# Row sums of the attention weights taken over pairs of tiles, added on VectorE first

## Chip, cores and metric

One Trainium2 chip, all 8 cores, one launch. Each core computes 1024 of the 8192 rows (batch x position) of the output; the cores don't talk to each other. The metric is the device time in microseconds (us) of the slowest core.

## The reference

One transformer layer, postnorm: strictly causal attention with 16 query heads over one shared key/value head, layer norm of the sum with the input, then a gated FFN with a Walsh-Hadamard transform of the hidden layer, and a second layer norm. Of it the attention is what matters here:

```python
q = (q_input @ Wq.T + bq).reshape(B, T, 16, 128).transpose(0, 2, 1, 3)   # B=2, T=4096
k = q_input @ Wk.T + bk                                                  # 128 wide, one head
v = q_input @ Wv.T + bv
mask = pos[None, :] < pos[:, None]
scores = jnp.einsum('bhtd,bsd->bhts', q, k) * scale
scores = jnp.where(mask[None, None, :, :], scores, NEG_BIG)
attn = jax.nn.softmax(scores, axis=-1)
...
out = jnp.einsum('bhts,bsd->bhtd', attn, v)
```

The softmax's denominator is the sum over s of exp(score); the kernel subtracts no maximum.

## The kernel before

The program is written out by hand: `em.op(engine, fn, waits)` appends an instruction to one engine's list ("t" TensorE, "v" VectorE, "s" ScalarE, "g" and "y" the GpSimd and SyncE queues for DMAs) and gives back a token, the value of that engine's semaphore after it. The lists are replayed in that order, so each engine runs its instructions in program order, and a wait holds all that stands behind it in its list. `inc=False` gives an instruction no token.

Stages in order: keys and values with W2T transforms (`p0_step`) woven in, queries, attention, output projection, first norm, FFN up, FFN down, second norm. All matmuls but those of `p0_step` go through line 177, whatever they compute; those of `p0_step` through 179.

The attention stage runs from about 334 to 1092 us. It loops over k = 0..7 (blocks of 128 queries) and g = 0..3 (groups of 4 heads): 32 groups, here counted by (k, g). A group works on 4(k+1) tiles; a tile is 128 keys by 512 columns (4 heads x 128 queries), held transposed with the keys on the partitions. The stage has 576 tiles. For each tile:

- QK: a matmul of kT and qT into one of two PSUM banks (of four, once the 64 `p0_step`s are done, from k=4 on);
- for the last four tiles of a group, those on the diagonal, a mask is added in PSUM on VectorE (L430);
- ScalarE takes the exp into a slot of `pbuf`, bf16, 128x512 (L433), six slots in turn;
- AV: a matmul of vP and the slot, accumulated over the group in bank 2 or 3;
- RS: a matmul of the one-column ONEC and the slot, accumulated in bank 4, row 0: the row sum.

AV and RS of a tile are issued two tiles behind its QK (`pend`). At the end of a group the last two are drained, and VectorE runs r1 (L446), r3 (L450), r4 (L452) and r5 (L454) on the row sum: it is split in two bf16 parts in RB2. What follows from it, `fin`, is issued in the next group, at it == 2, behind QK(2) and ahead of AV(0): two matmuls b1 and b2 that broadcast the two parts over the partitions (they wait for r3 and r5), the reciprocal on VectorE (L471) and the multiplication of the group's AV sum with it (L475). After the drain each group calls `p0_step` twice until the 64 are used up; at an odd step VectorE moves its results out of PSUM (L244), at an even one ScalarE (L240).

`pbuf` is laid out as eight slots of 1 KB, of which six are used. `pbuf_rd[slot]` holds the token for which the next exp into the slot waits.

Of the kernel before, what the change touches and what calls it, by code (L numbers as in the profile page):

```python
# [55 lines left out]
def _mx(*toks):  # L56
    d = {}

    def add(u):
        if u[0] in "gy":  # L60
            k = (u[0], ((u[1] // 16) - 1) % NL)
        else:
            k = u[0]
        if d.get(k, 0) < u[1]:
            d[k] = u[1]

    for t in toks:
        if not t:
            continue
        if isinstance(t, list):  # L70
            for u in t:
                if u:
                    add(u)
        else:
            add(t)
    return [((k[0] if isinstance(k, tuple) else k), v) for k, v in d.items()]


def build_program():
# [23 lines left out]
    em = EM()  # L103

    import contextlib
    with contextlib.ExitStack() as stack:
# [16 lines left out]
        pb = [ent(nc.psum_tensor("pb%d" % i, [128, 512], F32)) for i in range(8)]  # L123
# [32 lines left out]
        pbuf = [vb(O_PB + i * 1024, 512) for i in range(8)]  # L156
# [15 lines left out]
        ONEC = CB[:, 320:321]  # L172
        ONER = CB[0:1, 320:448]

        def MM(e, out, lhsT, rhs, start, stop, tp=None):
            if tp is None:
                return e.matmul(out, lhsT, rhs, start=start, stop=stop,  # L177
                                skip_group_check=True)
            return e.matmul(out, lhsT, rhs, start=start, stop=stop,  # L179
                            skip_group_check=True, tile_position=tp)  # L180

        tCB = em.op("y", lambda e: e.dma_start(CB[:], CONSTI[:]))
# [8 lines left out]
        for cc in range(4):  # L191
            sl = slice(cc * 512, cc * 512 + 512)
            tw = em.op("y", lambda e, sl=sl: e.dma_start(RR[0:1, 0:512], BOR[0:1, sl]),
                       waits=_mx(rr_rd))
            t1 = em.op("v", lambda e, sl=sl: e.tensor_sub(RR[0:1, 512:1024], RR[0:1, 0:512], BO2[0:1, sl]),
                       waits=_mx(tw, tBOh, last))
            rr_rd = t1
            last = em.op("v", lambda e, cc=cc: e.tensor_copy(BO2[0:1, 2048 + cc * 512:2048 + cc * 512 + 512], RR[0:1, 512:1024]),
                         waits=_mx(t1))
# [73 lines left out]
        for blk in range(8):  # L273
# [4 lines left out]
                waits=_mx(xtb_rd[sl]))  # L278
            pk = pb[sl]
            mmk = None  # L280
            for c in range(DC):
# [4 lines left out]
                    waits=_mx(tl, tWK, ps_tok[sl]) if c == 0 else (),  # L286
# [3 lines left out]
                waits=_mx(mmk, tBK))  # L290
# [4 lines left out]
            for c in range(DC):  # L295
# [4 lines left out]
                    waits=_mx(tWV, ps_tok[2 + sl]) if c == 0 else (),  # L300
# [4 lines left out]
                waits=_mx(mmv, tBV, vT_rd[sl]))  # L305
            ps_tok[2 + sl] = tev
            for st in range(4):
# [6 lines left out]
                    waits=_mx(tev, tCB, ps_tok[bank]))  # L314
                tevt = em.op("s", lambda e, pt=pt, sig=sig: e.copy(
                    vP[:, sig * 128:sig * 128 + 128], pt[:, 0:128]),
                    waits=_mx(mmt))
# [16 lines left out]
        for oq in range(4):  # L334
            sl = oq % 2
            tl = em.op("g", lambda e, sl=sl, oq=oq: e.dma_start(wqb[sl], WQS[oq]),
                       waits=_mx(wq_rd[sl]))
            for ot in range(4):
# [3 lines left out]
                for c in range(DC):  # L342
                    for th in range(2):
# [5 lines left out]
                            waits=_mx(tl, tXTOWN, q_ps_rd[bset + th]) if c == 0 else (),  # L349
# [29 lines left out]
        attnT_wr = []  # L379
        sig_ctr = 0  # L380
        first_attnT = True
        st3 = {"rb_rd": rb_rd, "rb2_rd": rb2_rd, "fin": None}

        qctr = 0
        for k in range(J):
            for g in range(NG):
                if p0_state["i"] >= 64 and len(QKB) == 2:
                    QKB = (0, 1, 6, 7)
                    qk_rd[6] = ps_tok[6]
                    qk_rd[7] = ps_tok[7]  # L390
                    qctr = 0
                avbank = 2 + (g % 2)
                avp = pb[avbank]
                rs_mm = None
                pend = []
                niter = (k + 1) * 4
                it = 0

                def emit_avrs(slot, sig, first, last_av, texp,
                              avp=avp, avbank=avbank):  # L400
                    em.op("t", lambda e, avp=avp, slot=slot, sig=sig,
                          first=first, last_av=last_av: MM(
                        e, avp[:], vP[:, sig * 128:sig * 128 + 128], pbuf[slot],
                        first, last_av),
                        waits=_mx(texp, tVP, av_rd[avbank] if first else None),
                        inc=False)
                    rs = em.op("t", lambda e, slot=slot, first=first,
                               last_av=last_av: MM(
                        e, pb[4][0:1, :], ONEC, pbuf[slot], first, last_av),
                        waits=_mx(rs_rd, tCB) if first else ())  # L410
                    pbuf_rd[slot] = rs
                    return rs

                for c in range(k + 1):
                    for q4 in range(4):
                        sig = 4 * c + q4
                        bank = QKB[qctr % len(QKB)]
                        qctr += 1
                        slot = sig_ctr % 6
                        sig_ctr += 1  # L420
                        qp = pb[bank]
                        rhs = qT.rearrange("p (h x) -> p h x", x=1024)[
                            :, 4 * g:4 * g + 4, k * 128:k * 128 + 128]
                        mm = em.op("t", lambda e, qp=qp, sig=sig, rhs=rhs: MM(
                            e, qp[:], kT[:, sig * 128:sig * 128 + 128], rhs,
                            True, True),
                            waits=_mx(tKT, tQT, qk_rd[bank]))
                        dep = mm
                        if c == k:
                            dep = em.op("v", lambda e, qp=qp, q4=q4: e.tensor_add(  # L430
                                qp[:], qp[:], maskP[:, q4 * 512:q4 * 512 + 512]),
                                waits=_mx(mm, tMask))
                        texp = em.op("s", lambda e, qp=qp, slot=slot: e.activation(  # L433
                            pbuf[slot], qp[:], AF.Exp, scale=SC),
                            waits=_mx(dep, pbuf_rd[slot]))
                        qk_rd[bank] = texp
                        if it == 2 and st3["fin"] is not None:
                            st3["fin"]()
                            st3["fin"] = None
                        if len(pend) == 2:  # L440
                            rs_mm = emit_avrs(*pend.pop(0))
                        pend.append((slot, sig, it == 0, it == niter - 1, texp))
                        it += 1
                while pend:
                    rs_mm = emit_avrs(*pend.pop(0))
                r1 = em.op("v", lambda e: e.tensor_scalar_add(RR[0:1, 0:512], pb[4][0:1, :], 1e-30),  # L446
                           waits=_mx(rs_mm, rr_war[0]))
                rr_war[0] = None
                rs_rd = r1
                r3 = em.op("v", lambda e: e.tensor_copy(RB2[0:1, 0:512], RR[0:1, 0:512]),  # L450
                           waits=_mx(r1, st3["rb2_rd"][0]))
                r4 = em.op("v", lambda e: e.tensor_sub(RR[0:1, 512:1024], RR[0:1, 0:512], RB2[0:1, 0:512]),  # L452
                           waits=_mx(r3))
                r5 = em.op("v", lambda e: e.tensor_copy(RB2[0:1, 512:1024], RR[0:1, 512:1024]),  # L454
                           waits=_mx(r4, st3["rb2_rd"][1]))
                rsl = (k * NG + g) % 2
                dst = attnT.rearrange("p (h x) -> p h x", x=1024)[
                    :, 4 * g:4 * g + 4, k * 128:k * 128 + 128]

                def make_fin(avp=avp, avbank=avbank, rsl=rsl, dst=dst,  # L460
                             rs_mm=rs_mm, r3=r3, r5=r5, fat=first_attnT,
                             qlm=q_last_mm):
                    def fin():
                        em.op("t", lambda e: MM(
                            e, pb[5][:], ONER, RB2[0:1, 0:512], True, False),
                            waits=_mx(r3, st3["rb_rd"]), inc=False)
                        b2 = em.op("t", lambda e: MM(
                            e, pb[5][:], ONER, RB2[0:1, 512:1024], False, True),
                            waits=_mx(r5))
                        st3["rb2_rd"] = [b2, b2]  # L470
                        vrec = em.op("v", lambda e, rsl=rsl: e.reciprocal(  # L471
                            recB[rsl], pb[5][:]),
                            waits=_mx(b2, recB_rd[rsl]))
                        st3["rb_rd"] = vrec
                        tv = em.op("v", lambda e, avp=avp, rsl=rsl, dst=dst: e.tensor_mul(  # L475
                            dst, avp[:], recB[rsl]),
                            waits=_mx(rs_mm, vrec, qlm if fat else None))
                        av_rd[avbank] = tv
                        recB_rd[rsl] = tv
                        attnT_wr.append(tv)  # L480
                    return fin

                st3["fin"] = make_fin()
                first_attnT = False
                p0_step()
                p0_step()
# [430 lines left out]
```

How the kernel before makes its waits and increments, by code:

```python
            def run(eng):  # L791
                lastw = {}
                def wait_tok(sc, val):
                    if sc in "gy":
                        n = val // 16
                        l = (n - 1) % NL
                        lv = 16 * ((n - 1) // NL + 1)
                        key = (sc, l)
                        if lastw.get(key, -1) < lv:
                            eng.wait_ge(lanes[sc][l], lv)
                            lastw[key] = lv
                    else:
                        if lastw.get(sc, -1) < val:
                            eng.wait_ge(sems[sc], val)
                            lastw[sc] = val
                for fn, ws, tok in em.ops[eng_char]:
                    if ANALYZE is not None:
                        ANALYZE(eng_char, fn, ws, tok)
                    for (sc, val) in ws:
                        wait_tok(sc, val)
                    if tok is not None and tok[0] in "gy":
                        n = tok[1] // 16
                        if n > NL:
                            wait_tok(tok[0], 16 * (n - NL))
                    ins = fn(eng)
                    if tok is not None:
                        if tok[0] in "gy":
                            n = tok[1] // 16
                            ins.then_inc(lanes[tok[0]][(n - 1) % NL], 16)
                        else:
                            ins.then_inc(sems[tok[0]], 1)
```

## Time and profile before

| | us |
|---|---|
| median of 3 runs | 2852.98 |
| the runs | 2852.71 to 3084.56 |
| the profiled execution | 2852.75 |
| its span, slowest core (first to last instruction) | 2851.2 |
| spans of the eight cores | 2840.8 to 2851.2 |

The profile shows the slowest core, 6. "PE" is a matmul on TensorE, "DVE" VectorE, "ACT" ScalarE. Duration of a matmul is from its start to a modelled end; the next one starts earlier, so the pace is read from the starts. "[0.70 <-DVE RB L450]" is the idle time of that engine ahead of the row and what ended it. "PEclk" is the granted TensorE clock as a share of its upper level: 1.00 is 2.4 GHz, 0.50 is 1.2 GHz.

### The profile page before, as it was taken

Reading aid. Unit: us, or ns where it says so; the run is one execution under the profiler, and the core shown is the slowest. Engines: PE = TensorE matmul, PEld = TensorE weight load, DVE = VectorE, ACT = ScalarE, POOL = GpSimd, SP = SyncE. Lnnn points to the kernel's source line nnn. Section 1 sums busy time; section 2 is a strip of 40 time slices with the busy share of each in tenths; the row PEclk is TensorE's granted clock in tenths of the full one; section 3 lists DMA queues with packets and bytes.
Section 4 is the critical chain, followed back from the end, with each engine's and each line's share of the span. In section 5 each row is a group of like instructions: output and inputs, shape, how many; then the busy total and the mean of one; then the engine's idle time right before and its main releaser. Section 6 shows DMA issues by size and latency. Waiting matters only on the chain.

```text
span 2851.2 us, 27832 instructions; the slowest of 8 cores (2840.8 to 2851.2 us)
## 1 busy us (share of the span) xinstructions
PE 2407.6 (84%) x9884; PEld 911.2 (32%) x10080; DVE 552.1 (19%) x768; ACT 647.7 (23%) x1131; POOL 162.8 (6%) x304
## 2 busy tenths in 40 slices
PE   3778758788889897957999999999999997979793
PEld 1233211112212222323444444444444443434341
DVE  1111346544332321131000000000000000010002
ACT  1222223445555551033111111111111100000001
POOL 1111101100000000000000000000000000000000
PEclk8799957889989998978999999999999998989896
DMA  8875554430000001122222212222222145446453
GB/s 235 235 210 155 168 165 118 113 91 18 1 1 0 1 1 59 60 103 86 69 67 69 71 67 68 73 67 67 74 67 67 52 140 148 144 138 199 133 153 126
DMA packets 96460, 276.69 MB, mean 97 GB/s; under 512 B 11716, under 2 KB 11844, under 8 KB 91976
## 3 DMA queue, kind: packets, MB, share of 16 engines
q0 software_dynamic: 37968, 156.26, 18.4%
q1 hardware_dynamic: 58360, 118.65, 13.5%
q8 instruction: 86, 1.41, 0.2%
q14 instruction: 46, 0.38, 0.0%
HBM read 224.54 MB, written 50.33 MB: 96 GB/s over the span
## 4 chain that ended last, share of the span: by engine, by line
PE 77%; DMA 7%; ACT 5%; DVE 5%; issue 5%; ACTq 0%; POOL 0%; DVEq 0%; SPq 0%; POOLq 0%
PE pb L177 75%; DMA GA<-XBT 2%; PE pb L179 2%; DMA GA<-X1S 2%; ACT GA L677 1%; ACT GA L433 1%; DVE pb L430 1%; DMA W2P<-GA 1%; ACT GA L240 1%; DVE GA L244 1%; DMA GA<-W2P 1%; DVE GA L471 1%; ACT GA L558 1%; DVE GA L737 0%; DVE RR L452 0%
## 5 line engine op out<-in xcount | busy, mean ns | idle before, releaser
L177 PE MATMUL pb<-GA 128*128 128x512 bf16 x8382 | 2045.4, 390 | 211.9 <-DVE GA L737 50.1
L177 PEld LDWEIGHTS pb<-GA 128*128 128x128 bf16 x8576 | 798.9, 99 | 1327.8 <-issue 505.2
L433 ACT ACTIVATE GA<-pb 128x512 bf16<-128x512 f32 x576 | 339.1, 597 | 336.0 <-PE pb L177 239.0
L177 PE MATMUL pb<-GA,CB 128*1 128x512 bf16 (+1 forms) x702 | 275.2, 406 | 13.7 <-issue 6.0
L677 ACT ACTIVATE GA<-pb 128x512 bf16<-128x512 f32 x128 | 69.6, 594 | 840.6 <-PE pb L177 840.5
L657 DVE TENSOR_TENSOR GA<-GA,pb 128x512 bf16<-128x512 f32 x128 | 82.3, 683 | 902.8 <-ACT GA L654 883.6
L179 PE MATMUL pb<-GA,CB 64*64 64x512 bf16 x512 | 107.9, 444 | 85.4 <-ACT GA L240 55.2
L177 PEld LDWEIGHTS pb<-GA,CB 128*1 128x1 bf16 (+1 forms) x704 | 58.1, 82 | 278.2 <-issue 263.4
L430 DVE TENSOR_TENSOR pb<-pb,GA 128x512 f32<-128x512 f32 x128 | 88.6, 698 | 296.8 <-PE pb L177 289.2
L244 DVE CAST GA<-pb 128x512 bf16<-128x512 f32 x128 | 82.6, 686 | 279.7 <-PE pb L179 278.4
L737 DVE TENSOR_TENSOR GA<-pb,GA 128x512 f32<-128x512 f32 x32 | 20.6, 686 | 497.3 <-PE pb L177 435.3
L471 DVE RECIPROCAL GA<-pb 128x512 f32<-128x512 f32 x32 | 107.4, 3357 | 36.2 <-PE pb L177 36.2
L179 PEld LDWEIGHTS pb<-GA,CB 64*64 64x64 bf16 x512 | 31.6, 108 | 159.2 <-issue 159.0
L240 ACT CAST GA<-pb 128x512 bf16<-128x512 f32 x128 | 68.7, 588 | 52.7 <-PE pb L179 31.1
L177 PE MATMUL pb<-CB,GA 128*128 128x128 bf16 x160 | 22.0, 285 | 59.9 <-ACT GA L565 36.8
L654 ACT ACTIVATE GA<-pb 128x512 f32<-128x512 f32 x128 | 70.0, 609 | 0.0
L617 POOL DMA_DIRECT2D GA<-W1S x64 | 34.0, 531 | 615.6 <-PE pb L177 605.1
L217 POOL DMA_DIRECT2D GA<-W2T x64 | 33.2, 518 | 543.2 <-PE pb L179 505.8
L762 ACT ACT_TABLE_LOAD x1 | 1.3, 1283 | 268.3 <-DVE LNS L760 268.3
L762 ACT ACTIVATE LNS<-LNS,EPSB 128x1 f32<-128x1 f32 x8 | 2.3, 292 | 252.9 <-DVE LNS L760 252.9
L619 POOL DMA_DIRECT2D GA<-W3S x64 | 34.0, 531 | 395.5 <-PE pb L177 392.7
L177 PE MATMUL pb<-RB,CB 1*128 1x512 bf16 x64 | 28.9, 500 | 26.8 <-DVE RB L454 14.9
(48 smaller groups left out, 382.8 us busy)
## 6 DMA issues: line engine op xcount, KB each, us to landing
GA<-W2P SPq DMA_DIRECT2D x256, 256.0 KB, 2.7
GA<-W2T POOLq DMA_DIRECT2D x128, 256.0 KB, 4.9
W2P<-GA SPq DMA_DIRECT2D x128, 256.0 KB, 5.9
GA<-W1S POOLq DMA_DIRECT2D x64, 512.0 KB, 3.7
GA<-W3S POOLq DMA_DIRECT2D x64, 512.0 KB, 3.7
GA<-XBT POOLq DMA_DIRECT2D x8, 2048.0 KB, 16.6
GA<-WQS POOLq DMA_DIRECT2D x4, 2048.0 KB, 11.8
GA<-XOWN SPq DMA_DIRECT2D x1, 8192.0 KB, 37.9
```

Source lines behind the costliest of these rows:

```text
L177: return e.matmul(out, lhsT, rhs, start=start, stop=stop, skip_group_check=True)
L179: return e.matmul(out, lhsT, rhs, start=start, stop=stop, skip_group_check=True, tile_position=tp)
L240: te = em.op("s", lambda e, ps=ps, stb=stb, q4=q4: e.copy(stb[:, q4 * 512:q4 * 512 + 512], ps[:]), waits=_mx(tm, p0_state["st_rd"][j % 2]))
L244: te = em.op("v", lambda e, ps=ps, stb=stb, q4=q4: e.tensor_copy(stb[:, q4 * 512:q4 * 512 + 512], ps[:]), waits=_mx(tm, p0_state["st_rd"][ ...
L430: dep = em.op("v", lambda e, qp=qp, q4=q4: e.tensor_add(qp[:], qp[:], maskP[:, q4 * 512:q4 * 512 + 512]), waits=_mx(mm, tMask))
L433: texp = em.op("s", lambda e, qp=qp, slot=slot: e.activation(pbuf[slot], qp[:], AF.Exp, scale=SC), waits=_mx(dep, pbuf_rd[slot]))
L471: vrec = em.op("v", lambda e, rsl=rsl: e.reciprocal(recB[rsl], pb[5][:]), waits=_mx(b2, recB_rd[rsl]))
L617: tl1 = em.op("g", lambda e, sl=sl, tau=tau: e.dma_start(w1b[sl], W1S[tau]), waits=_mx(w1_rd[sl]))
L619: tl3 = em.op("g", lambda e, sl=sl, tau=tau: e.dma_start(w3b[sl], W3S[tau]), waits=_mx(w3_rd[sl]))
L654: ts_ = em.op("s", lambda e, pg=pg, sl=sl, th=th: e.activation(silu[sl][:, th * 512:th * 512 + 512], pg[:], AF.Silu), waits=_mx(g_toks[th] ...
L657: tvm = em.op("v", lambda e, pl=pl, sl=sl, th=th: e.tensor_mul(hbuf[sl][:, th * 512:th * 512 + 512], silu[sl][:, th * 512:th * 512 + 512], ...
L677: ev = em.op("s", lambda e, pg=pg, tau=tau, th=th: e.activation(hid[:, tau * 1024 + th * 512:tau * 1024 + th * 512 + 512], pg[:], AF.Ident ...
```

## The change

RS is no longer taken of each tile. When AV of the second tile of a pair has been issued, VectorE adds the two `pbuf` slots into a third, slot 6 or 7 in turn, and one RS is taken of that sum. The sum is bf16, as are its inputs. The RS waits for the addition; the addition waits for both exps and for the RS that last read its slot. A slot of the first six is given free when both the addition and that RS are done. 288 RS matmuls stay, 288 additions are new. Nothing else is changed.

```diff
-        st3 = {"rb_rd": rb_rd, "rb2_rd": rb2_rd, "fin": None}
+        st3 = {"rb_rd": rb_rd, "rb2_rd": rb2_rd, "fin": None, "pc": 0}
+        pbuf6_rd = [None, None]
...
+                rsp = []
...
                         waits=_mx(texp, tVP, av_rd[avbank] if first else None),
                         inc=False)
-                    rs = em.op("t", lambda e, slot=slot, first=first,
-                               last_av=last_av: MM(
-                        e, pb[4][0:1, :], ONEC, pbuf[slot], first, last_av),
-                        waits=_mx(rs_rd, tCB) if first else ())
-                    pbuf_rd[slot] = rs
+                    rsp.append((slot, texp, first, last_av))
+                    rs = None
+                    if len(rsp) == 2:
+                        (sa, ta_, fa, la_), (sb, tb_, fb, lb_) = rsp
+                        del rsp[:]
+                        psl = 6 + (st3["pc"] % 2)
+                        st3["pc"] += 1
+                        va = em.op("v", lambda e, sa=sa, sb=sb, psl=psl: e.tensor_add(
+                            pbuf[psl], pbuf[sa], pbuf[sb]),
+                            waits=_mx(ta_, tb_, pbuf6_rd[psl - 6]))
+                        rs = em.op("t", lambda e, psl=psl, fa=fa, lb_=lb_: MM(
+                            e, pb[4][0:1, :], ONEC, pbuf[psl], fa, lb_),
+                            waits=_mx(va, rs_rd, tCB) if fa else _mx(va))
+                        pbuf6_rd[psl - 6] = rs
+                        pbuf_rd[sa] = _mx(rs, va)
+                        pbuf_rd[sb] = _mx(rs, va)
                     return rs
...
                         if len(pend) == 2:
-                            rs_mm = emit_avrs(*pend.pop(0))
+                            rs_mm = emit_avrs(*pend.pop(0)) or rs_mm
...
                 while pend:
-                    rs_mm = emit_avrs(*pend.pop(0))
+                    rs_mm = emit_avrs(*pend.pop(0)) or rs_mm
```

## Rows read from the trace of the kernel before

**Rows 1.** The page, part 4, the chain that ended last, by engine.
```profile
PE 77%; DMA 7%; ACT 5%; DVE 5%; issue 5%; ACTq 0%; POOL 0%; DVEq 0%; SPq 0%; POOLq 0%
```
**Rows 2.** Busy time by window, attention stage: from:to, length, engines, PEclk, DMA share, GB/s.
```profile
334.00:1092.00 758.00, 634.14 (x2007) 140.91 (x2046) 324.30 (x383) 373.48 (x640) 31.12 (x61) 0.85 0.20 56
```
**Rows 3.** Groups by line and form: operation, shapes, count | busy, mean ns | idle before.
```profile
L177 PE MATMUL pb<-GA,CB 128*1 128x512 bf16 x576 | 237.4, 412 | 10.8 <-issue 6.0 <-ACT GA L433 1.8
...
L430 DVE TENSOR_TENSOR pb<-pb,GA 128x512 f32<-128x512 f32 x128 | 88.6, 698 | 296.8 <-PE pb L177 289.2
...
L452 DVE TENSOR_TENSOR RR<-RR,RB 1x512 f32<-1x512 f32 x32 | 21.7, 679 | 3.3
...
L450 DVE CAST RB<-RR 1x512 bf16<-1x512 f32 x32 | 13.3, 415 | 3.3
```
**Rows 4.** Timeline, all engines, mid-group (k=7): start, duration, engine, operation, count.
```profile
1000.02 0.38 PE L177 MATMUL pb<-GA,CB 128*1 128x512 bf16 x1
...
1000.33 0.60 PE L177 MATMUL pb<-GA 128*128 128x512 bf16 x2
1000.81 0.60 ACT L433 ACTIVATE GA<-pb 128x512 bf16<-128x512 f32 x1 [0.25 <-PE pb L177]
...
1000.86 0.38 PE L177 MATMUL pb<-GA,CB 128*1 128x512 bf16 x1
```
**Rows 5.** Timeline, first masks on the diagonal of that group.
```profile
1018.56 1.54 DVE L430 TENSOR_TENSOR pb<-pb,GA 128x512 f32<-128x512 f32 x2 [19.39 <-PE pb L177]
```
**Rows 6.** Timeline, end of that group and head of the next.
```profile
1023.41 0.82 PE L177 MATMUL pb<-GA 128*128 128x512 bf16 x3
1023.59 0.68 DVE L446 TENSOR_SCALAR RR<-pb 1x512 f32<-1x512 f32 x1 [1.68 <-PE pb L177]
...
1025.67 0.41 DVE L454 CAST RB<-RR 1x512 bf16<-1x512 f32 x1
...
1026.23 0.58 PE L177 MATMUL pb<-RB,CB 1*128 1x512 bf16 x1 [0.93 <-DVE RB L454]
...
1026.92 3.36 DVE L471 RECIPROCAL GA<-pb 128x512 f32<-128x512 f32 x1 [0.83 <-PE pb L177]
...
1028.76 0.58 PE L177 MATMUL pb<-GA,CB 128*1 128x512 bf16 x1
...
1030.24 0.58 PE L177 MATMUL pb<-GA,CB 128*1 128x512 bf16 x1
1030.38 0.69 DVE L475 TENSOR_TENSOR GA<-pb,GA 128x512 bf16<-128x512 f32 x1
```
**Rows 7.** Busy time by window, columns as in rows 2; two low stretches and k=4.
```profile
995.50:998.90 3.40, 3.40 (x9) 0.51 (x8) 3.29 (x2) 1.19 (x2) 0.00 (x0) 0.50 0.03 7
...
1026.20:1033.00 6.80, 6.77 (x14) 1.03 (x14) 4.05 (x2) 1.85 (x4) 0.00 (x0) 0.50 0.00 0
...
705.30:742.90 37.60, 33.44 (x115) 8.11 (x116) 14.67 (x20) 22.70 (x39) 0.00 (x0) 1.00 0.00 1
```
**Rows 8.** Timeline of VectorE: reciprocals and r1 in groups of k=2, 4, 7.
```profile
546.38 3.36 DVE L471 RECIPROCAL GA<-pb 128x512 f32<-128x512 f32 x1 [1.94 <-PE pb L177]
...
559.13 0.68 DVE L446 TENSOR_SCALAR RR<-pb 1x512 f32<-1x512 f32 x1 [1.68 <-PE pb L177]
...
702.12 3.36 DVE L471 RECIPROCAL GA<-pb 128x512 f32<-128x512 f32 x1 [0.62 <-PE pb L177]
...
720.55 0.68 DVE L446 TENSOR_SCALAR RR<-pb 1x512 f32<-1x512 f32 x1 [1.68 <-PE pb L177]
723.67 3.36 DVE L471 RECIPROCAL GA<-pb 128x512 f32<-128x512 f32 x1 [0.62 <-PE pb L177]
...
740.63 0.68 DVE L446 TENSOR_SCALAR RR<-pb 1x512 f32<-1x512 f32 x1 [1.68 <-PE pb L177]
...
995.01 3.36 DVE L471 RECIPROCAL GA<-pb 128x512 f32<-128x512 f32 x1 [0.62 <-PE pb L177]
...
1056.71 0.68 DVE L446 TENSOR_SCALAR RR<-pb 1x512 f32<-1x512 f32 x1 [1.68 <-PE pb L177]
```

## The prediction

> **What bounds the kernel now.** I read the page first. Its chain of work that ended last lies on TensorE [rows 1], so a change off TensorE counts only through what TensorE waits for. The busy time by window comes next: the attention stage holds 758 of 2851 us, TensorE busy in 634 of them, ScalarE in 373, VectorE in 324 [rows 2]. The groups by form give the price of each operation there, among them the 576 row-sum matmuls of which the change takes half away [rows 3]. Then the timeline, in four places. In the middle of a group TensorE is the pace: a tile (scores QK, weighted values AV, row sum RS) recurs every 0.84 us, and the exp takes 0.60 of it [rows 4]. On the diagonal four masks stand on VectorE, and 5.03 us pass from the first mask to r1 [rows 5, 6]. Between groups TensorE waits for r1 to r5, runs the two broadcast matmuls of `fin` and goes on, while VectorE works off the reciprocal (3.36 us) and the multiplication (0.69) behind which nobody waits [rows 6]. In some of these places the granted clock falls to 1.2 GHz for 3.4 or 6.8 us, and a tile then takes 1.48 us instead of 0.84; in others it stays at 2.4 GHz [rows 7, 6].
>
> **What a removed row sum is worth.** RS starts, QK starts 0.31 later, AV follows, and the next RS starts 0.53 after that QK [rows 4]. Three QKs in a row take 0.82 with a last duration of 0.39, so matmuls of one shape stand 0.216 apart [rows 6]. Each change of shape to the one-column weights and back costs about 0.09 more. A tile without its RS is therefore 0.844 - 0.31 - 0.31 + 0.216 = 0.44, a pair with one RS 0.844 + 0.44 = 1.286, or 0.643 per tile. One removed RS gives 0.40 us, 288 of them 116 us, if nothing waits. At the low clock I scale the tile: 1.48 x 0.643 / 0.844 = 1.13 us. ScalarE at 0.60 stays just under that pace.
>
> **What the new addition costs.** The trace has no addition of bf16 with bf16. Its nearest rows at 512 elements: TENSOR_TENSOR f32 in SBUF 679 ns, with PSUM 698, CAST f32 to bf16 415 [rows 3]. The addition reads 2+2 bytes and writes 2 per element, as the cast reads 4 and writes 2, while the f32 addition moves 12; I take 0.415 us and keep 0.68 for the upper end. Less than 0.415 no row suggests. With 0.415 the sum below comes to 2924 us, with 0.68 to 2969.
>
> Beside that, the Trainium skill ("VectorE: DVE Perf Modes", The perf-mode tier table) puts tensor_tensor on bf16 in SBUF at two elements a cycle, 1224 ns for 2048 elements; less three quarters of the elements, that is an estimate of 424 ns here. By it the sum would be 2925 us. No row of this trace shows a two-source operation at that rate.
>
> In the middle of a group the addition is hidden. Handover from matmul to exp is 0.48 (1000.33 to 1000.81), the exp 0.60 [rows 4], a handover from ScalarE to VectorE 0.10 (my estimate; TensorE to VectorE takes about as long as TensorE to ScalarE, and VectorE to TensorE 0.15), the addition 0.415, and one to TensorE 0.15 (L454 ends 1026.08, broadcast 1026.23) [rows 6]: 1.75 us after its QK the sum is there. RS(pair) stands 1.82 us behind the QK of its second tile (one pair period of 1.286, plus 0.53). 0.07 us to spare, and at 0.68 a wait of 0.19 per pair.
>
> **Where it isn't hidden: at the head of a group.** `fin` is emitted at it == 2, and its reciprocal and multiplication enter VectorE's queue. The first pair's addition is emitted at it == 3, behind both, and VectorE works in order. RS(0,1) stands in TensorE's queue right behind AV(1), and behind it QK(4), so all of the group. Counted from the start of the reciprocal: multiplication from 3.46 to 4.15 [rows 6], addition to 4.6, RS(0,1) at 4.75. TensorE has by then done AV(0), QK(3), AV(1), four matmuls' work with the broadcast, and idles for about 3 us. In the kernel before it works through at that place. QK(4) follows at 5.29 (0.31 scaled to the low clock).
>
> The clock: a gap of this size next to that of r1 to r5 leaves it at 1.2 GHz. Before, low stretches were 3.4 or 6.8 us long [rows 7]; I take 5.1 us from RS(0,1), so until 9.85. In it (9.85 - 5.29) / 1.13 = 4.0 tiles pass: QK(8) at 9.85, and from there 0.643 per tile.
>
> **And on the diagonal.** With T the start of the first mask (QK + 0.49; the masks take 0.70): second mask T+0.66 to 1.36, then the addition of the pair before to 1.74, its RS 1.88 (TensorE waits 1.4 us), the next two QKs 2.19 and 2.62, masks 2.67 to 3.37 and 3.33 to 4.03, the second addition to 4.41, its RS 4.55, last exp 4.13 to 4.73, last AV 5.07, last addition 4.83 to 5.25, last RS 5.39, r1 5.88. Before it was 5.03. So from QK of the first masked tile to r1: 0.49 + 5.88 = 6.37. pbuf is no new wait: a slot is used again six tiles on, a pair frees it after three.
>
> **The sum.** Reciprocal to r1 for U unmasked tiles, after: 9.85 + (U - 8) x 0.643 + 6.37, and for U = 4 5.29 + 6.37 = 11.7. Before, from the reciprocal and r1 of [rows 8] and [rows 6]: k=2 12.75; k=4 18.43 and 16.96, mean 17.7; k=7 28.58 and 29.79, mean 29.2; the others a tile rate of 0.844 away from a neighbour.
> U = 4 (k=1): 11.7 against 9.4, +2.3. U = 8: 16.2 against 12.75, +3.45. U = 12: 18.8 against 16.1, +2.7. U = 16: 21.35 against 17.7, +3.65. U = 20: 23.9 against 22.4, +1.5. U = 24: 26.5 against 25.8, +0.7. U = 28: 29.05 against 29.2, -0.15. Together 14.15, times four groups: +56.5. k=0: three groups with a `fin` whose last mask waited for the reciprocal already, +0.35 each (0.10 + 0.415 + 0.15 less 0.31), +1. The saving of the row sums is inside these figures; every fourth tile is on a diagonal or in the low stretch, where it is eaten.
> To it: TensorE idles about 3 of the 5.9 us of the diagonal, so I let the clock fall there in half of the 28 groups, 0.8 us each (the last four matmuls twice as long): +11. The two broadcasts at the low clock, 0.2 us in 14 more groups: +3. Sum +71.5. The profiled execution ran 2852.75 us (span 2851.2; the median of the runs is 2852.98): 2924 us. The stages behind are not touched, and the W2T transforms (L179), whose VectorE casts stand ahead of the reciprocal, keep their place in each queue and so their price: 0.
>
> **The rivals.**
> A. The low stretch after the stall is always 3.4 us and none falls on the diagonal: 1.7 x (1 - 0.643/1.13) = 0.73 us in 24 groups less, 2852.75 + 57.5 - 17.5 = 2893. For it: of the two late groups shown one has the short stretch [rows 7]. Against: in those the work behind the broadcasts was without a gap, and here the stall lies in it.
> B. Not slower: the clock stays at 2.4 GHz through the stall. Then QK(4) comes at 5.06 and U = 4..28 give +2.0, +1.25, +0.5, +1.5, -0.7, -1.5, -2.3, times four +3, with k=0 +4: 2857. It decides at the head of each group. For it: one boundary at k=4 was crossed at 2.4 GHz [rows 7]. Against: that gap was 2 us, here there are two with 5 us of idling in 7.
> C. The addition takes 0.68: 0.26 more at the head, 0.52 on the diagonal, 28 times, 22 us; and 0.19 in the 120 pairs at full clock, 23 us: 2969. For it: each two-source row is at 679 or more. Against: the bytes moved.
> D. The reciprocal doesn't hold the sum up and the whole 116 us are gained: 2737. The program's order speaks against it; nothing for it.
>
> **How the numbers follow.** The forecast has 0.57, A 0.17, B 0.08, C 0.14, D 0.04. About 2% (2910 us) is what a measurement here can tell from no change. The forecast's own spread is 2900 to 2950, so one tenth of it lies within 2%, as do A and B: same 0.31. Faster 0.05, D and some of B. Slower 0.64. The range 2880 to 2975 takes in the forecast, A and C, and leaves out B and D.
>
> **What would show it right or wrong.** The mean of the new addition (415 ns). A wait of TensorE for it once per group of about 3 us behind the multiplication, 28 times, some 85 us in all, and two of 1 to 1.5 us on the diagonal. Tiles 1.29 us per pair in mid-group at 2.4 GHz. A granted clock of the attention stage under the 0.85 of before. Reciprocal to r1 near 16 us at k=2 and 29 at k=7. Wrong would be: no wait at the head (D), or a clock of 1.00 there (B). The stages behind should not change.

## The result, and the profile after

| | before | after |
|---|---|---|
| ratio to the kernel before | 1 | 1.0253 (95% interval 1.0225 to 1.028) |
| median of all runs, us | 2863.19 (10 runs) | 2926.68 (10 runs) |
| profiled execution, us | 2852.75 | 2930.88 |
| its span, slowest core, us | 2851.2 (core 6) | 2929.2 (core 1) |

The change makes the kernel 2.5% slower: 1.0253 times the 2852.98 us of the runs shown is 2925 us, where 2924 was predicted. In some runs the cores of one die show a lower granted clock and the time is longer, whatever the kernel; the ratios, here and below, leave these runs out.

The spans differ by 78 us and the whole runs by 72: eleven microseconds of the difference lie ahead of attention (first exp at 345.1 us here, at 334.2 before) where the program is the same. In this execution cores 0 and 1 were granted less clock there (PEclk, third from the end, is 0.70 in core 1 and 0.82 in core 2), and their first exp comes at 344.0 and 345.1 us, that of the other six at 322.3 to 335.8. Window 62 to 220 us, core 1 and then core 2:

```profile
62.00:220.00 158.00, 125.73 (x461) 45.29 (x462) 20.64 (x32) 38.03 (x83) 24.51 (x41) 0.70 0.75 213
```
```profile
62.00:220.00 158.00, 126.24 (x509) 47.74 (x508) 23.21 (x36) 39.39 (x85) 25.61 (x43) 0.82 0.77 216
```

From the first reciprocal to the last, attention takes 811.8 us instead of 744.4, 67.4 more; on the mean of the eight cores it is 68.7.

The chain of work that ended last, by engine and by line (compare [rows 1]): VectorE goes from 5% to 10%, and the reciprocal (L484, before L471) from 1% to 4%; it now stands second.

```profile
PE 74%; DVE 10%; DMA 6%; issue 5%; ACT 5%; DVEq 0%; ACTq 0%; POOL 0%; SPq 0%; POOLq 0%
PE pb L177 71%; DVE GA L484 4%; PE pb L179 2%; DVE pb L443 2%; DMA GA<-XBT 2%; DMA GA<-X1S 2%; ACT GA L690 1%; DVE GA L416 1%; ACT GA L240 1%; DMA W2P<-GA 1%; DVE GA L244 1%; DMA GA<-W2P 1%; ACT GA L571 1%; ACT GA L446 1%; DVE GA L750 0%
```

The windows of the kernel after (columns as in [rows 2]): the attention stage, then a stretch in k=0 and k=1, then two low stretches of k=7. TensorE has 66 us less work and the stage is 69 us longer; the granted clock over it falls from 0.85 to 0.74. From the first r1 to the last, 423 of 818 us are at 1.2 GHz, where it was 225 of 750.

```profile
345.00:1172.00 827.00, 568.50 (x1758) 139.38 (x1758) 432.00 (x670) 358.22 (x640) 30.89 (x61) 0.74 0.17 51
...
1101.10:1114.70 13.60, 8.88 (x19) 1.66 (x20) 7.80 (x12) 4.18 (x8) 0.00 (x0) 0.50 0.00 0
...
1138.60:1148.90 10.30, 6.96 (x16) 1.51 (x16) 5.37 (x6) 2.98 (x5) 0.00 (x0) 0.50 0.00 0
346.70:524.20 177.50, 108.44 (x278) 21.62 (x277) 99.88 (x137) 48.88 (x86) 16.35 (x32) 0.50 0.48 147
```

Groups by form and the waits of TensorE in that kernel: the halved row sums with the idle time in front of them (10.8 us before, [rows 3]), the addition (L416), and the sum of TensorE's waits for an addition, with their number and the longest. The first row sums of the 28 groups from k=1 on hold 101 us of that idle time, 3.34 to 3.98 us each.

```profile
L177 PE MATMUL pb<-GA,CB 128*1 128x512 bf16 x288 | 127.4, 443 | 183.2 <-DVE GA L416 180.9
...
L416 DVE TENSOR_TENSOR GA<-GA 128x512 bf16<-128x512 bf16 x288 | 119.5, 422 | 209.3 <-PE pb L177 119.0
```
```profile
PE pb L177 <- DVE GA L416: 180.9, 94, 4.0
```

The head of a group of k=7, timeline of all engines. It answers to [rows 6]. The two additions at 1111.27 come when the multiplication L488 is done; RS(0,1) follows at 1111.83, after 3.35 us in which TensorE had nothing.

```profile
1106.51 0.58 PE L177 MATMUL pb<-RB,CB 1*128 1x512 bf16 x1 [0.72 <-DVE RB L467]
...
1107.02 1.46 PE L177 MATMUL pb<-GA 128*128 128x512 bf16 x3
...
1107.20 3.36 DVE L484 RECIPROCAL GA<-pb 128x512 f32<-128x512 f32 x1 [0.83 <-PE pb L177]
...
1110.66 0.69 DVE L488 TENSOR_TENSOR GA<-pb,GA 128x512 bf16<-128x512 f32 x1
1111.27 0.75 DVE L416 TENSOR_TENSOR GA<-GA 128x512 bf16<-128x512 bf16 x2
...
1111.83 0.59 PE L177 MATMUL pb<-GA,CB 128*1 128x512 bf16 x1 [3.35 <-DVE GA L416]
```

Mid-group in the same kernel: row sums at 1122.58, 1123.86 and 1125.26, so a pair takes 1.28 and 1.40 us in turn.

```profile
1122.58 0.38 PE L177 MATMUL pb<-GA,CB 128*1 128x512 bf16 x1
...
1123.86 0.38 PE L177 MATMUL pb<-GA,CB 128*1 128x512 bf16 x1
...
1125.26 0.38 PE L177 MATMUL pb<-GA,CB 128*1 128x512 bf16 x1
```

The diagonal of that kernel, TensorE, and VectorE's first mask and r1 (it answers to [rows 5, 6]): two waits of 1.23 us for additions that stand behind masks, and 5.73 us from first mask to r1 instead of 5.03. These two waits stand in each group from k=2 on; in k=1 they are of 0.85 us.

```profile
1131.79 0.38 PE L177 MATMUL pb<-GA,CB 128*1 128x512 bf16 x1 [1.23 <-DVE GA L416]
1132.10 1.04 PE L177 MATMUL pb<-GA 128*128 128x512 bf16 x4
1134.36 0.38 PE L177 MATMUL pb<-GA,CB 128*1 128x512 bf16 x1 [1.23 <-DVE GA L416]
```
```profile
1130.02 1.30 DVE L443 TENSOR_TENSOR pb<-pb,GA 128x512 f32<-128x512 f32 x2 [0.95 <-PE pb L177]
...
1135.75 0.68 DVE L459 TENSOR_SCALAR RR<-pb 1x512 f32<-1x512 f32 x1 [0.63 <-PE pb L177]
```

### The profile page after: what moved, and what is told of

The parts are those of the page before. It is cut to its first block, busy times and chain, and to the rows that moved or that the text cites. A ratio compares the mean times of both kernels' runs of the same rounds, so it can differ in the third digit from the quotient of the medians.

```text
span 2929.2 us, 28624 instructions; the slowest of 8 cores (2904.3 to 2929.2 us)
## 1 busy us (share of the span) xinstructions
PE 2363.5 (81%) x9792; PEld 911.1 (31%) x9792; DVE 660.0 (23%) x1056; ACT 632.7 (22%) x1131; POOL 162.1 (6%) x304
## 3 DMA queue, kind: packets, MB, share of 16 engines
q1 hardware_dynamic: 58360, 118.65, 12.7%
## 4 chain that ended last, share of the span: by engine, by line
PE 74%; DVE 10%; DMA 6%; issue 5%; ACT 5%; DVEq 0%; ACTq 0%; POOL 0%; SPq 0%; POOLq 0%
PE pb L177 71%; DVE GA L484 4%; PE pb L179 2%; DVE pb L443 2%; DMA GA<-XBT 2%; DMA GA<-X1S 2%; ACT GA L690 1%; DVE GA L416 1%; ACT GA L240 1%; DMA W2P<-GA 1%; DVE GA L244 1%; DMA GA<-W2P 1%; ACT GA L571 1%; ACT GA L446 1%; DVE GA L750 0%
## 5 line engine op out<-in xcount | busy, mean ns | idle before, releaser
L177 PE MATMUL pb<-GA 128*128 128x512 bf16 x8576 | 2056.4, 395 | 175.7 <-DVE GA L750 45.9
L177 PEld LDWEIGHTS pb<-GA 128*128 128x128 bf16 x8576 | 820.3, 100 | 1322.0 <-issue 486.7
L446 ACT ACTIVATE GA<-pb 128x512 bf16<-128x512 f32 x576 | 323.9, 596 | 411.9 <-PE pb L177 291.6
L177 PE MATMUL pb<-GA,CB 128*1 128x512 bf16 (+1 forms) x416 | 165.7, 423 | 186.0 <-DVE GA L416 180.9
L690 ACT ACTIVATE GA<-pb 128x512 bf16<-128x512 f32 x128 | 69.6, 595 | 840.8 <-PE pb L177 840.8
L179 PE MATMUL pb<-GA,CB 64*64 64x512 bf16 x512 | 119.9, 500 | 75.8 <-ACT GA L240 49.9
L416 DVE TENSOR_TENSOR GA<-GA 128x512 bf16<-128x512 bf16 x288 | 119.5, 422 | 209.3 <-PE pb L177 119.0
L177 PEld LDWEIGHTS pb<-GA,CB 128*1 128x1 bf16 (+1 forms) x416 | 35.3, 85 | 360.9 <-issue 346.1
L750 DVE TENSOR_TENSOR GA<-pb,GA 128x512 f32<-128x512 f32 x32 | 20.6, 686 | 495.1 <-PE pb L177 437.3
L484 DVE RECIPROCAL GA<-pb 128x512 f32<-128x512 f32 x32 | 107.4, 3358 | 39.8 <-PE pb L177 39.8
L179 PEld LDWEIGHTS pb<-GA,CB 64*64 64x64 bf16 x512 | 32.8, 114 | 160.2 <-issue 160.0
L177 PE MATMUL pb<-CB,GA 128*128 128x128 bf16 x160 | 22.2, 289 | 59.4 <-ACT GA L578 45.0
## 6 DMA issues: line engine op xcount, KB each, us to landing
GA<-WQS POOLq DMA_DIRECT2D x4, 2048.0 KB, 12.7
```

The lines of the kernel that those rows point to most:

```text
L177: return e.matmul(out, lhsT, rhs, start=start, stop=stop, skip_group_check=True)
L179: return e.matmul(out, lhsT, rhs, start=start, stop=stop, skip_group_check=True, tile_position=tp)
L416: va = em.op("v", lambda e, sa=sa, sb=sb, psl=psl: e.tensor_add(pbuf[psl], pbuf[sa], pbuf[sb]), waits=_mx(ta_, tb_, pbuf6_rd[psl - 6]))
L446: texp = em.op("s", lambda e, qp=qp, slot=slot: e.activation(pbuf[slot], qp[:], AF.Exp, scale=SC), waits=_mx(dep, pbuf_rd[slot]))
L484: vrec = em.op("v", lambda e, rsl=rsl: e.reciprocal(recB[rsl], pb[5][:]), waits=_mx(b2, recB_rd[rsl]))
L690: ev = em.op("s", lambda e, pg=pg, tau=tau, th=th: e.activation(hid[:, tau * 1024 + th * 512:tau * 1024 + th * 512 + 512], pg[:], AF.Ident ...
```

## Experiments

Each was timed in rounds against the kernel before. The ratios stand together first (line numbers shift a little from run to run: L177 is L179 where lines were added ahead of it, and the addition stands at L416, L419, L420, L423 or L430):

| run | what | ratio | 95% interval |
|---|---|---|---|
| the change | | 1.0253 | 1.0225 to 1.028 |
| e1_head | first pair of each group single | 0.999 | 0.9978 to 1.0002 |
| e2_diag | last three pairs single | 1.017 | 1.0147 to 1.0193 |
| e3_both | both | 0.9893 | 0.9875 to 0.9911 |
| e4_after_norecip | the change without the reciprocal | 0.9949 | 0.993 to 0.9969 |
| e5_before_norecip | before without the reciprocal | 0.9922 | 0.9899 to 0.9946 |
| e6_addonly | before with idle additions | about 1.00 | none given |
| e8_addtwice | the change, additions twice | 1.0584 | 1.0566 to 1.0602 |
| e9_lag0 | more buffers, row sum in place | 1.0272 | 1.0223 to 1.0322 |
| e10_lag1 | row sum one pair later | 0.9899 | 0.9842 to 0.9956 |
| e7_defer | row sum four pairs later | 0.9658 | 0.9642 to 0.9673 |
| e11_quad | sums of four, row sum two fours later | 0.9644 | 0.9616 to 0.9672 |

### Where the loss is: e1_head, e2_diag, e3_both

Within `emit_avrs`, ahead of the pairing, each run with one of the three conditions ("..." stands for what is left out, here and below):

```diff
+                    if sig < 2:                          # e1_head
+                    if sig >= niter - 6:                 # e2_diag
+                    if sig < 2 or sig >= niter - 6:      # e3_both
+                        rs = em.op("t", ... pb[4][0:1, :], ONEC, pbuf[slot], first, last_av),
+                            waits=_mx(rs_rd, tCB) if first else ())
+                        pbuf_rd[slot] = rs
+                        return rs
                     rsp.append((slot, texp, first, last_av))
```

> The changed kernel, but in each group the first pair (tiles 0 and 1) keeps its two single row sums and no addition; all other pairs are added. Theory (the row sum of the first pair waits for the reciprocal, and TensorE stands behind it): that wait goes, and of the wait for the next pair's addition only about 0.6 us is left at 1.2 GHz (row sum due 4.1 us behind the start of the reciprocal, sum there at 4.75), up to 2.3 us at 2.4 GHz. About 2.3 us less in 28 groups, 65 us: 0.978 of the changed kernel, 1.002 of the kernel before (about 2860 us). Rival (the load of 288 additions on VectorE or the diagonal is what costs): 32 of 288 additions less, so at most 20 us less, 1.018 of the kernel before.

> The changed kernel, but the last three pairs of each group (the six tiles whose additions would stand among the masks) keep single row sums. Theory: first mask to r1 falls from 5.9 back to 5.0 us, the low clock inside the diagonal goes, the head of the group is as slow as in the changed kernel: 25 to 35 us less, 1.015 of the kernel before (about 2896 us). Rival (the head costs nothing, the diagonal everything): 75 us less, about 1.00.

> Both edits together: single row sums for the first pair and the last three pairs of each group, 164 of 288 additions stay (k=0 and k=1 have none). Theory: both waits are gone and the gain of the middle stays, 0.40 us per removed row sum less what the second pair still waits: 0.990 to 0.995 of the kernel before (2825 to 2840 us). Rival (the additions cost something of their own wherever they stand): 1.00 or more.

The head is the loss: 32 of 288 additions taken away give 2.6% (75 us; 65 were expected), and the kernel is level with the one before. The diagonal gives 0.8% (24 us). Together they give 3.6%, within the noise the sum of the two, and the kernel is then 1.1% faster than the one before, with 168 additions left (the 164 of the expectation was a miscount). The waits of TensorE for an addition, in e1_head, e2_diag and e3_both (where the pair behind the first still waits), show the same: with the diagonal mended what stays is about one long wait per group, with both mended less than a sixth of the waits of the change.

```profile
PE pb L177 <- DVE GA L423: 93.7, 88, 2.3
```
```profile
PE pb L177 <- DVE GA L423: 101.8, 31, 4.0
```
```profile
PE pb L177 <- DVE GA L423: 27.0, 27, 2.3
```

### That it is the reciprocal: e4_after_norecip, e5_before_norecip

```diff
-                        vrec = em.op("v", lambda e, rsl=rsl: e.reciprocal(
-                            recB[rsl], pb[5][:]),
+                        vrec = em.op("v", lambda e, rsl=rsl: e.tensor_scalar_mul(
+                            recB[rsl], pb[5][:], 1e-10),
```

> The changed kernel with the reciprocal replaced by a multiplication with a constant (1e-10), about 0.69 us instead of 3.36; this leaves the softmax's division out. Theory: the head wait is as long as the reciprocal makes it: it falls by 2.67 us in 28 groups, and 2.67 us in the three groups of k=0 whose last mask stands behind it; 83 us less than the changed kernel, some more by shorter low stretches: about 2840 us, 0.995 of the kernel before. Rival (the wait is for something else, exps or handovers): under 10 us less.

> The kernel before with the reciprocal replaced by a multiplication with a constant (1e-10), which leaves the softmax's division out. Theory: in that kernel nobody waits behind the reciprocal but the last mask of k=0, so 3 times 2.67 us: 0.997, about 2845 us. Rival (the reciprocal costs time in the kernel before too): 0.98 or less, and then the difference of the two kernels without it says less on the change.

The changed kernel gains 3.0% (87 us) and lands where expected; TensorE's waits for additions fall from 180.9 to 97.5 us and the longest from 4.0 to 1.3. The wait at the head falls by just what the shorter instruction saves, from 3.35 to 0.68 us or from 3.98 to 1.32, in the 28 groups together from 101 to 26 us. The sum of waits, and the head of a group of k=7:

```profile
PE pb L177 <- DVE GA L416: 97.5, 93, 1.3
```
```profile
1025.57 0.69 DVE L484 TENSOR_SCALAR GA<-pb 128x512 f32<-128x512 f32 x1 [0.62 <-PE pb L177]
...
1027.53 0.58 PE L177 MATMUL pb<-GA,CB 128*1 128x512 bf16 x1 [1.32 <-DVE GA L416]
```

The kernel before gains 0.8% (22 us), nearly three times what was expected. The three groups of k=0 give their 2.2 us each; in the groups of k=1 to k=3 the time from that instruction to r1 is also shorter, by up to 2.7 us and 15 us together, and in those of k=4 longer, 4 us together; no wait on the reciprocal stands in the trace for either. Their low stretches lie elsewhere; why was not tested. So of the 87 us, about 22 come in the kernel before too, and about 65 are the change's own. Without the reciprocal the change is level with the kernel before (0.9949 against 0.9922, intervals overlapping). That the waits on the diagonal and what is left at the head eat the removed row sums fits the 97.5 us of waits, but was not shown by a run of its own.

### That the additions by themselves cost nothing: e6_addonly, e8_addtwice

```diff
# e6_addonly, on the kernel before
                     pbuf_rd[slot] = rs
+                    rsp.append((slot, texp))
+                    if len(rsp) == 2:
...
+                        va = em.op("v", ... e.tensor_add(pbuf[psl], pbuf[sa], pbuf[sb]),
+                            waits=_mx(ta_, tb_, sumw[psl - 6]))
+                        sumw[psl - 6] = va
+                        pbuf_rd[sa] = _mx(rs, va)
+                        pbuf_rd[sb] = _mx(rs, va)
# e8_addtwice, on the changed kernel
                             waits=_mx(ta_, tb_, pbuf6_rd[psl - 6]))
+                        va = em.op("v", ... e.tensor_add(pbuf[psl], pbuf[sa], pbuf[sb]), waits=_mx(va))
```

> The kernel before with the 288 additions issued at the places where the changed kernel has them, their sums read by nobody; all 576 single row sums stay. It measures what VectorE's part costs alone. Theory: little, since TensorE waits for no sum; the masks of the diagonal stand behind additions for about 0.1 to 0.4 us a group: 1.001 to 1.005. Rival (the additions hold the masks, r1 or the buffers of the exps so much that the row sums are not needed for the loss): 1.02 or more.

> The changed kernel with each addition done twice, one behind the other, on the same buffers: 0.42 us and a handover of 0.1 more for each pair. Theory (the addition is just hidden in mid-group, with 0.07 us to spare, and counts once at the head and twice on the diagonal): 1.56 us in 28 groups, 44 us, and 0.45 us in 120 pairs at full clock, 54 us: about 3025 us, 1.06 of the kernel before. Rival (there is room in mid-group): only the 44 us, 2970 us, 1.041.

Of e6_addonly only two runs compare, 2848.57 and 2852.89 us; five of the kernel before beside it are 2852.49 to 2858.54. No interval can be given, but nothing near the rival's 1.02 shows. 288 additions that nobody on TensorE waits for cost nothing that can be told. e8_addtwice, 1.0584 for 1.06 expected: there is no room in mid-group. A timeline of TensorE in it shows, in this group, row sums that wait 0.43 us every second pair in mid-group, and 1.76 instead of 1.23 on the diagonal:

```profile
1202.49 0.38 PE L177 MATMUL pb<-GA,CB 128*1 128x512 bf16 x1 [0.43 <-DVE GA L419]
...
1203.92 0.38 PE L177 MATMUL pb<-GA,CB 128*1 128x512 bf16 x1
...
1210.24 0.38 PE L177 MATMUL pb<-GA,CB 128*1 128x512 bf16 x1 [1.76 <-DVE GA L419]
```

The total agrees better than its terms. A pair in mid-group takes 1.64 us on the mean instead of 1.35, so the second addition costs 0.28 there and not 0.45; but from k=2 on the kernel spends 402 us at 1.2 GHz, where the change spends 268.

### Mending the order instead: e7_defer, e9_lag0, e10_lag1

The sums get six buffers of their own and the exps twelve; AV of the second tile gives the token that frees the exps' buffers; the row sums wait in a list and are issued LAG pairs later, the rest at the group's end. LAG is 4, 0 and 1.

```diff
-        pbuf = [vb(O_PB + i * 1024, 512) for i in range(8)]
+        pbuf = ([vb(O_PB + i * 1024, 512) for i in range(8)]
+                + [vb(O_KSQ + i * 1024, 512) for i in range(4)])
+        psum = [vb(O_KSQ + 4096 + i * 1024, 512) for i in range(6)]
...
+                        inc=(sig % 2 == 1))
...
+                        pbuf_rd[sa] = _mx(av, va)
+                        pbuf_rd[sb] = _mx(av, va)
+                        rsq.append((psl, fa, lb_, va))
+                    if len(rsq) > LAG:
+                        rs = emit_rs(*rsq.pop(0))
...
                 while pend:
                     rs_mm = emit_avrs(*pend.pop(0)) or rs_mm
+                while rsq:
+                    rs_mm = emit_rs(*rsq.pop(0))
```

> The changed kernel with all 288 additions, but the row sum of a pair is issued four pairs later on TensorE (the rest at the end of the group), with six buffers for sums and twelve for exps, so that nobody on TensorE waits for a sum that is late. Theory: the head wait of about 3 us and the waits of the diagonal go while all removed row sums count: 0.20 us for each of 448 unmasked tiles, 90 us, less 0.3 us in each of 32 groups, 10 us, against the kernel before: 0.972, about 2773 us. Rival (VectorE's own order is the limit, the exps wait for buffers behind the reciprocal, or ScalarE at 0.60 us per exp becomes the pace): 0.99 to 1.00.

> The kernel of the late row sums with the lateness set to none: twelve buffers for exps and six for sums, and the row sum right behind the second tile's AV as in the changed kernel. It parts the two edits of e7_defer. Theory (TensorE's order is what costs; buffers alone free nobody): as the changed kernel, 1.020 to 1.028. Rival (the buffers gave the gain): under 1.00.

> The same with the row sum one pair later. Theory: the row sum of the first pair is due 2.9 us behind the start of the reciprocal at 1.2 GHz and its sum is there at 4.75, so 1.9 us of the wait of 3.3 is left, and the waits of the diagonal are mostly gone: about 75 us less than the changed kernel, 0.995 to 1.000. Rival (any lateness at all is enough, since what costs is the handover and not the reciprocal): 0.966 as with four pairs.

With the same 288 additions and the same 288 row sums, four pairs later, the kernel is 3.4% faster than the one before (2757.20 us median) and 5.8% faster than the change. The buffers alone give nothing (e9_lag0 1.0272), one pair later gives more than half of it (e10_lag1, 100 us less than the change where 75 were expected; TensorE's waits for additions are down to 60.9 us, one in each of the 28 groups). The head of a group of k=7 in e7_defer: TensorE goes on, 14 matmuls in a row from 946.92, while VectorE works off the reciprocal, the multiplication and then five additions together; of all its waits for an addition 0.8 us are left. What it waits for now is above all the exp.

```profile
944.98 3.36 DVE L496 RECIPROCAL GA<-pb 128x512 f32<-128x512 f32 x1 [0.83 <-PE pb L179]
...
946.92 3.90 PE L179 MATMUL pb<-GA 128*128 128x512 bf16 x14 [0.22 <-issue]
...
949.05 1.77 DVE L420 TENSOR_TENSOR GA<-GA 128x512 bf16<-128x512 bf16 x5
...
950.74 0.38 PE L179 MATMUL pb<-GA,CB 128*1 128x512 bf16 x1
```
```profile
PE pb L179 <- ACT GA L456: 69.4, 104, 3.9
...
PE pb L179 <- DVE GA L420: 0.8, 1, 0.8
```

The gain, 3.42%, or 98 us, is more than the 80 expected: reciprocal to r1 in the groups of k=7 is 21.1 to 22.3 us against 28.6 to 29.8, so about 7.5 less where 5.6 - 0.3 was worked out. It doesn't come behind the first mask of the diagonal: from there to r1 is 5.42 us in k=4 to 7, where it was 5.03. What is seen is less time at 1.2 GHz: 82 us from k=2 on instead of 126. At 0.43 us for each microsecond (my estimate, 1 - 0.643/1.13) that is about 19 us. In k=0 and k=1 the kernel is at 1.2 GHz nearly throughout and loses some 10 us against the one before. The rest was not singled out.

### One step further: e11_quad

```diff
# on e7_defer, LAG = 2
-                        rsq.append((psl, fa, lb_, va))
+                        quad.append((psl, fa, lb_, va))
+                        if len(quad) == 2:
...
+                            vq = em.op("v", ... e.tensor_add(psum[p0_], psum[p0_], psum[p1_]),
+                                waits=_mx(v0_, v1_))
+                            psum_rd[p1_] = vq
+                            rsq.append((p0_, f0_, l1_, vq))
```

> All 576 exps summed by fours: two pair sums are added again on VectorE (432 additions), 144 row sums, issued two fours later. Theory: another 144 row sums less at 0.40 us each is 58 us at 2.4 GHz, but a tile of 0.54 us is under the 0.60 of an exp, whose starts stand 0.5 apart at best, so about half of it: 0.955 to 0.960 of the kernel before. Rival (VectorE, 0.32 us of additions per tile and the masks and reciprocal beside it, becomes the pace): 0.966 or more.

0.9644 against 0.9658, the intervals overlap: half the row sums again give nothing that can be told. In mid-group a four takes 2.39 us (row sums at 954.45 and 956.83, rounded), 0.60 per tile, against 0.64 in e7_defer (954.57, 955.85: 1.28 per pair). But the granted clock over the stage is lower, 0.77 against 0.83. Windows 340 to 995 us, e11_quad and e7_defer:

```profile
340.00:995.00 655.00, 508.00 (x1608) 133.10 (x1608) 479.12 (x807) 350.22 (x636) 30.66 (x60) 0.77 0.20 64
```
```profile
340.00:995.00 655.00, 510.24 (x1725) 139.94 (x1756) 424.99 (x669) 353.68 (x639) 30.77 (x60) 0.83 0.21 65
```

Neither reading of the expectation was quite met: VectorE at 479 of 655 us is not the pace, and against the gain of mid-group stands more time at 1.2 GHz (153 us from k=2 on, 82 in e7_defer). That the one causes the other was not tested.

## Why the prediction was right

**By its groups.** Reciprocal to r1, mean of the groups of each k (three with k=0), in us:

| k | before | predicted | after |
|---|---|---|---|
| 0 | 6.7 | 7.0 | 7.4 |
| 1 | 9.4 | 11.7 | 13.3 |
| 2 | 12.7 | 16.2 | 15.9 |
| 3 | 16.4 | 18.8 | 18.8 |
| 4 | 17.7 | 21.35 | 20.6 |
| 5 | 22.3 | 23.9 | 24.2 |
| 6 | 25.75 | 26.5 | 26.4 |
| 7 | 29.2 | 29.05 | 29.6 |

Over all groups these differences are 63 us; the sum predicted 57.5, and 11 more for a clock that falls on the diagonal. Two rows of each of k=1 and k=2, reciprocal and next r1:

```profile
447.91 3.36 DVE L484 RECIPROCAL GA<-pb 128x512 f32<-128x512 f32 x1 [2.23 <-PE pb L177]
461.23 0.68 DVE L459 TENSOR_SCALAR RR<-pb 1x512 f32<-1x512 f32 x1 [1.42 <-PE pb L177]
```
```profile
538.52 3.36 DVE L484 RECIPROCAL GA<-pb 128x512 f32<-128x512 f32 x1 [2.23 <-PE pb L177]
554.48 0.68 DVE L459 TENSOR_SCALAR RR<-pb 1x512 f32<-1x512 f32 x1 [0.63 <-PE pb L177]
```

**The addition.** Taken at 0.415, measured 0.422 (0.415 to 0.427). Rival C (0.68) falls. The Trainium skill's rate for tensor_tensor on bf16 ("VectorE: DVE Perf Modes", The perf-mode tier table), from which 424 ns was estimated, agrees with the trace's 422.

**The head.** RS(0,1) at 4.75 us behind the reciprocal's start, measured 4.63 in each of the 28 groups; the idling about 3 us and 85 in all, measured 3.35 to 3.98 and 101 in all. That this wait is the larger part of the loss is shown from three sides: the first pair taken out (e1_head), the reciprocal taken out (e4, e5), the row sum moved (e7, e9, e10). Rival D falls with them. Rival B falls too: a low stretch stands at each of the 28 heads. It was taken to end 9.85 us behind the reciprocal's start; from k=2 on it ends 7.5 to 10.7 us behind, 8.9 on the mean.

**The diagonal.** 5.88 predicted, 5.73 measured; two waits of 1 to 1.5 us, measured 1.23 and 1.23. Where the clock falls there, first mask to r1 takes 6.51 us, the 0.8 more that was assumed. But it does so in 6 of the 24 groups from k=2 on, not in half of them. One of the two low stretches above is such a case (it begins at 1101.10, r1 is at 1103.87), the other begins behind r1. Rival A, by which none falls on the diagonal and the stretch behind the stall lasts 3.4 us, is thus right for 18 of these 24 on the first point, and near it for 11 on the second (2.9 to 3.7 us).

**Mid-group.** 1.286 per pair predicted; 1.28 and 1.40 in turn measured. The 0.07 us to spare were not there: every second pair takes 0.12 longer. In e10_lag1, where the sum is due a pair later, each takes 1.28, so it is the addition that TensorE waits for; which handover is longer than estimated was not singled out. Some 120 pairs at 0.06 make 7 us that the sum didn't have.

**What was mis-sized, and cancelled.** Each is an estimate from the times above.

- The low stretches behind the stall are 0.9 us shorter than assumed from k=2 on: about 10 us less.
- The clock on the diagonal: 6 groups from k=2 on at 0.8 us make 5. But k=1, predicted at 2.4 GHz on the diagonal, is at 1.2 GHz throughout (the window 346.7 to 524.2 above), 1.6 us more in four groups. Together that is 11, the figure of the forecast, and by luck: half of the groups was wrong.
- The diagonal itself is 0.16 us shorter in 24 groups, 4 us less; mid-group is 7 us more, k=0 1 us more.
- r1 to the next reciprocal was held to change by the two broadcasts alone, 3 us. From k=4 on it didn't grow at all. It grew by 9 us in k=1 to 3, where the `p0_step`s lie between (8.82 us in k=1 where it had been 7.35 to 8.14), and of the time from the first r1 to that of the last group of k=1, 155 us are at 1.2 GHz instead of 99. Against it, it was 4 us shorter in k=0, where the wait for the write of W2P was shorter.

With these the 71.5 us of the sum become 67 to 68, which is what attention took more; the ratio's 72 us hold a few more, and where they lie was not singled out. The forecast is better than its terms, whose errors are up to 10 us each way.

## What to carry to other kernels

Work taken off the engine that sets the end gives nothing if the engine that takes it over has a long instruction in its queue, and the first engine's own queue has the use of the result right behind. Look for the longest instruction of the engine that gets the new work (here 3.36 us, nobody waiting behind it before) and ask who will now stand behind it; here that cost 75 us, in a change that had 116 us to gain at the most. Before giving up such a change, move the use later and give the results buffers: the same instructions in another order, with more buffers, went from 2.5% slower to 3.4% faster.

## What the runs showed of the hardware

- A row sum costs TensorE nearly twice its own 0.216 us. Matmuls start 0.31 us apart where the stationary operand changes between 128 columns and one, and 0.216 apart where it doesn't; with a row sum removed, a pair went from 1.69 to 1.28 us.
- TensorE stayed at 1.2 GHz for 177.5 us on end while busy in 108.4 of them (window 346.7 to 524.2), and in the last 100 of these us, in k=1, none of its idle times was over 3.35 us; in the kernel before, the granted clock rose five times in the same groups (k=0 and k=1).
- With the reciprocal made short, the kernel before gained 22 us though only 7 are at places where somebody waits for it. Why stays open.
